# A new order of work, per-bank score waits and slot-wise restacking in two six-layer attention stacks

## What is computed

```
for i in range(NL):                        # NL = 6, B = 2, L = 512, 16 heads of 8 features
    xn = _adaln(x, noise_emb, n1_w[i], n1_b[i])
    q, k, v = split(xn @ qkv_w[i].T);  q, k = _rope(q), _rope(k)
    x = x + _attn(q, k, v, src_mask) @ so_w[i].T           # self attention, 512 keys
    xn = _adaln(x, noise_emb, n2_w[i], n2_b[i])
    q = _rope(xn @ cq_w[i].T);  k = _rope(context @ ck_w[i].T);  v = context @ cv_w[i].T
    x = x + _attn(q, k, v, ctx_mask) @ co_w[i].T           # cross attention, 154 keys
    xn = _adaln(x, noise_emb, n3_w[i], n3_b[i])
    x = x + (gelu(xn @ f1_w[i].T + f1_b[i]) @ f2_w[i].T + f2_b[i])   # DFF = 512
```

## Time and profile before

| | |
|---|---|
| three runs | 3256.78, 3264.88, 3266.14 us; median 3264.88 |
| profiled execution | 3269.45 us, span 3267.6 us |
| busy share of the span | TensorE 89%, VectorE 64%, ScalarE 59%, GpSimd 25% |
| granted TensorE clock | 0.960 of full speed |
| first stack | about 676 to 1877 us |
| second stack | about 1940 to 3145 us |

### The profile page before, as it was taken

How to read it: one execution, slowest core, us unless ns; L and a number is a source line. 1 busy time by engine, 2 the same in 40 slices (tenths; PEclk the granted TensorE clock), 3 DMA queues, 4 the chain that set the end, 5 groups by cost and what they waited for, 6 DMA issues and landing times.

```text
span 3267.6 us, 44859 instructions
## 1 busy us (share of the span) xinstructions
PE 2898.7 (89%) x15719; PEld 1046.8 (32%) x15719; DVE 2098.5 (64%) x3625; ACT 1911.9 (59%) x2677; POOL 828.0 (25%) x1327
## 2 busy tenths in 40 slices
PE   7998999969989898998989857989899898998988
PEld 2474344322323223232222222222323222232237
DVE  4316788548485775948577378577495766848523
ACT  5533444428677584766758435758476575857632
POOL 0003556532222222222222111222222222222201
PEclk9999999979999999999999877999999999999998
DMA  1101000001101111111111101111111111111130
GB/s 46 59 1 26 1 1 1 11 20 38 43 27 38 44 29 41 38 42 36 36 41 33 34 18 30 30 41 34 41 31 40 42 31 37 38 48 29 36 128 7
DMA packets 125514, 110.11 MB, mean 34 GB/s; under 512 B 49982, under 2 KB 116076, under 8 KB 125292
## 3 DMA queue, kind: packets, MB, share of 16 engines
q1 hardware_dynamic: 114924, 97.80, 10.2%
q10 hardware_dynamic: 10368, 9.44, 1.0%
HBM read 41.96 MB, written 0.52 MB: 13 GB/s over the span
## 4 chain that ended last, share of the span: by engine, by line
PE 68%; DVE 17%; ACT 5%; issue 4%; SPq 2%; POOL 2%; DMA 2%; ACTq 0%; DVEq 0%; POOLq 0%
PE ps L524 12%; DVE arena L813 8%; PE ps L469 7%; PE ps L498 3%; PE ps L641 3%; PE ps L656 3%; PE ps L598 3%; PE ps L541 3%; PE ps L1521 3%; PE ps L1509 2%; PE ps L532 2%; PE ps L584 2%; PE ps L553 2%; PE ps L573 2%; PE ps L1467 2%
## 5 line engine op out<-in xcount | busy, mean ns | idle before, releaser
L681 ACT ACTIVATE arena<-ps 128x1024 f32<-128x1024 f32 x960 | 934.6, 1022 | 245.9 <-PE ps L498 235.7
L813 DVE TENSOR_REDUCE arena<-ps 128x1 f32<-128x512 f32 x1536 | 963.9, 683 | 112.5 <-PE ps L469 103.3
L524 PE MATMUL ps<-arena 128*32 128x512 f32 x3840 | 503.2, 605 | 2.1 <-ACT arena L700 0.3
L469 PE MATMUL ps<-arena 49*128 49x512 bf16 x1536 | 309.3, 399 | 154.3 <-DVE arena L813 109.8
L815 DVE TENSOR_REDUCE arena<-ps 128x3 f32<-128x462 f32 (+1 forms) x576 | 305.4, 579 | 139.4 <-PE ps L476 119.0
L498 PE MATMUL ps<-arena 52*128 52x512 bf16 x1920 | 343.0, 385 | 29.8 <-DMA arena<-arena 9.3
L903 POOL TENSOR_TENSOR arena<-arena,zeros 128x16 bf16<-128x16 f32 x192 | 42.3, 220 | 1081.8 <-DVE arena L813 703.2
L469 PEld LDWEIGHTS ps<-arena 49*128 49x128 bf16 x1536 | 74.9, 93 | 545.7 <-DVE arena L813 474.7
L913 POOL TENSOR_TENSOR arena<-arena 128x512 f32<-128x512 f32 x96 | 122.1, 1272 | 388.5 <-ACT arena L713 385.2
L1586 ACT ACTIVATE arena<-ps 128x1024 f32<-128x1024 f32 x96 | 98.1, 1021 | 156.0 <-DVE ps L1671 152.6
L362 PE MATMUL ps<-consts 128*128 128x512 f32 x344 | 166.2, 608 | 23.7 <-DVE arena L2113 23.7
(11 more groups left out here) (389 smaller groups left out, 4351.9 us busy)
## 6 DMA issues: line engine op xcount, KB each, us to landing
arena<-arena SPq DMA_DIRECT2D x720, 64.0 KB
arena<-we_dram SPq DMA_DIRECT2D x24, 578.5 KB, 7.6
arena<-arena ACTq DMA_DIRECT2D x144, 64.0 KB
w<-weights_dram SPq DMA_DIRECT2D x26, 320.0 KB, 3.3
w<-weights_dram SPq DMA_DIRECT2D x13, 512.0 KB, 4.2
arena<-arena SPq DMA_DIRECT2D x384, 6.0 KB
arena<-arena SPq DMA_DIRECT2D x288, 19.2 KB
w<-weights_dram SPq DMA_DIRECT2D x39, 128.0 KB, 2.2
```

The lines of the kernel that those rows point to most:

```text
L469: pe.matmul(s_bank(slot + r), qst[b][rows, idx, P * qt:P * (qt + 1)], kst[b][rows, idx, :], start=True, stop=True).then_inc(s_full, 1)
L524: mm = pe.matmul(bank(7)[32 * j:32 * j + 32, :], v, prob[:, slot, j, :], start=(g % 2 == 0 and kt == 0), stop=(a == 0 and g % 2 == 1 and k ...
L681: act.activation(prob[:, chunk_no(b, a, g, kt) % NPROB, 2 * p:2 * p + 2, :], e_bank(slot).rearrange("p (j n) -> p j n", j=2), ACT.Exp, sca ...
L813: op = ve.tensor_reduce(nmax[:, g % 2, r, n:n + 1], s_bank(slot + r), AX.X, ALU.max, negate=True)
```

## The change

Seven edits, all in the stacks:

1. `st` has one item for each row slot, with two DMAs (four for `u` = 3), and a layer 392 items for 371. The DMAs are the same ones.
2. `ACT_STACKS` has twelve items of two DMAs: ScalarE issues 24 a layer for 12. It waits for the part that the slot needs, so also for the middle and low ones of GpSimd.
3. All places are new. The first score of a layer moves from place 0 to -6. Among the others: `out 1,1` (batch 1's cross output) stood three places before the first score and stands behind the sixth one; `sel 1,1,*` stand behind the second and third score; `f1 1,*` and `f2 1` move from places 13 to 21 to 30 to 34.
4. A self-attention `score` waits for its first bank ahead of the first product and for its second bank ahead of the second one.
5. Fillers: ten for nine, at other items; ahead of a score they wait for one bank only.
6. Other items may have fillers (`exp`, `tail`, `sel`, `proj`, `f2`); of these only two `exp` items have one.
7. On ScalarE and VectorE some pairs of waits of one instruction change their order.

```diff
-PER_LAYER = 371
+PER_LAYER = 392
-    ('score', 0, 0): [[0, 2, 3, 5, 6, 9, 11, 12], [14, 17, 18, 23, 25, 27, 28, 30], [36, 44, 50, 55, 57, 61, 63,
-        66], [69, 71, 77, 79, 82, 85, 89, 92]],
+    ('score', 0, 0): [[-6, -5, -2, 2, 3, 5, 7, 8], [11, 12, 16, 17, 21, 22, 25, 28], [31, 33, 36, 38, 40, 42,
+        44, 48], [56, 58, 71, 73, 74, 76, 82, 84]],
...
-    ('sel', 1): [[214, 254], [362, 364]],
+    ('sel', 1): [[220, 270], [389, 392]],
-    ('out',): [[156, 291], [265, 368]],
+    ('out',): [[177, 309], [278, 398]],
...
-    ('st', 0): [[-22, -2, -4], [-12, -5, -1], [188, 212, 210], [124, 160, 148]],
+    ('st', 0): [[-33, -12, -14, -34, -30, -31], [-23, -28, -19, -20, -15, -16], [203, 219, 214, 212, 208, 206],
+        [183, 145, 178, 129, 156, 153]],
...
-    ('f1',): [[304, 306], [384, 387]],
-    ('f2',): [313, 392],
+    ('f1',): [[319, 322], [422, 424]],
+    ('f2',): [328, 426],
...
-        def restack(eng, b, u, part):
-            for slot in slots_of(u, part):
-                for r in range(2):
...
+        def restack(eng, b, u, slot):
+            part = part_in(u, slot)
+            for r in range(2):
...
-        ACT_STACKS = (("st", 0, 1, 0), ("st", 1, 2, 0))
-        FILL = {("out", 0, 1): 3, ("out", 1, 1): 2, ("f1", 0, 0): 1, ("score", 1, 1, 0, 0): 2, ("center", 0, 2): 1}
+        ACT_STACKS = (("st", 0, 0, 0), ("st", 0, 0, 1), ("st", 0, 1, 1), ("st", 0, 1, 4), ("st", 0, 2, 1),
+                      ("st", 1, 0, 2), ("st", 1, 0, 3), ("st", 1, 1, 1), ("st", 1, 1, 2), ("st", 1, 1, 4),
+                      ("st", 1, 2, 3), ("st", 1, 2, 5))
+        FILL = {('exp', 0, 0, 0, 1, 0): 1, ('exp', 1, 1, 1, 0, 0): 1, ('out', 0, 1): 2, ('score', 0, 0, 1, 1):
+                1, ('score', 0, 0, 1, 3): 1, ('score', 0, 0, 1, 5): 1, ('score', 1, 1, 0, 0): 2, ('var', 0,
+                2): 1}
...
                 if it in FILL:
-                    pe.wait_ge(s_free, z.room("s", it, 2))
+                    pe.wait_ge(s_free, z.room("s", it, 1))
                     fill(it, s_bank(z.use("s", it)[0]))
...
-                pe.wait_ge(s_free, z.room("s", it, 2))
                 if a == 0:
                     idx, qt = 2 * g + n // 4, n % 4
                     for r in range(2):
                         rows = slice(64 * r, 64 * r + K_SCORE)
+                        pe.wait_ge(s_free, z.room("s", it, 1) if r == 0 else floor0(at - 1))
                         pe.matmul(s_bank(slot + r), qst[b][rows, idx, P * qt:P * (qt + 1)], kst[b][rows, idx, :],
                                   start=True, stop=True).then_inc(s_full, 1)
                     return
+                pe.wait_ge(s_free, z.room("s", it, 2))
...
-                    act.wait_ge(part_hi, z.after("hi", ("hi", b, u), it))
-                    restack(act, b, u, part)
+                    act.wait_ge((part_hi, part_mid, part_lo)[part_in(u, slot)], z.after("hi", ("hi", b, u), it))
+                    restack(act, b, u, slot)
```

More of the change, by code:

```diff
@@ new lines @@
+    ('sel', 0): [[139, 161], [299, 301]],
+    ('sel', 1): [[220, 270], [389, 392]],
+    ('inv', 0): [[146, 164], [300, 303]],
+    ('inv', 1): [[224, 271], [391, 393]],
+    ('out',): [[177, 309], [278, 398]],
+    ('center',): [[-59, 184, 311], [39, 284, 402]],
+    ('var',): [[-55, 188, 312], [43, 289, 407]],
+    ('apply',): [[-48, 194, 315], [46, 290, 412]],
+    ('proj',): [[-41, -36, 198, 86], [53, 57, 302]],
+    ('hi',): [[-35, -29, 200, 128], [59, 62, 304]],
+    ('st', 0): [[-33, -12, -14, -34, -30, -31], [-23, -28, -19, -20, -15, -16], [203, 219, 214, 212, 208, 206],
+        [183, 145, 178, 129, 156, 153]],
@@ L139 @@
+    ('st', 1): [[61, 70, 68, 60, 67, 81], [77, 78, 65, 89, 69, 90], [305, 313, 316, 306, 307, 308]],
+    ('ktail',): 211,
+    ('vals',): [4, 133, -7],
+    ('f1',): [[319, 322], [422, 424]],
+    ('f2',): [328, 426],
+    ('gain',): [-82, -13, 314],
+    ('biasf',): 291,
+    ('load',): {'cout': 419, 'cross': 350, 'ffn': 634, 'n0': 241, 'n1': 189, 'n2': 558, 'self': 259, 'sout':
+        346},
 }
@@ L175, in steps @@
     if kind == "st":
[L176 to L177 removed]
+        return {"c": 64} if item[2] == 3 else {("k" if item[2] == 1 else "q") + str(item[1]): 32}
     if kind == "load":
@@ L492, in exp @@
                 slot, at = z.use("e", it)
+                if it in FILL:
+                    pe.wait_ge(e_free, z.room("e", it, 1))
+                    fill(it, e_bank(slot)[:, 0:S])
                 if p == 0 and kt == 0:
@@ L589, in proj @@
                 slot, at = z.use("s", it)
+                if it in FILL:
+                    pe.wait_ge(s_free, z.room("s", it, 1))
+                    fill(it, s_bank(slot))
                 if u == 3:
@@ L964, in stack @@
             def stack(it):
-                _, b, u, part = it
+                _, b, u, slot = it
                 if it not in ACT_STACKS:
-                    sp.wait_ge((part_hi, part_mid, part_lo)[part], z.after("hi", ("hi", b, u), it))
-                    restack(sp, b, u, part)
+                    sp.wait_ge((part_hi, part_mid, part_lo)[part_in(u, slot)], z.after("hi", ("hi", b, u), it))
+                    restack(sp, b, u, slot)
             def load(it):
```

108 lines of the change are left out of this document (48 added, 60 removed), and 2 rows, old and new, of the table PLACES.

## The result

The changed kernel takes 3286.75 us (median of four runs, 3280.57 to 3296.74), the kernel before 3260.83 us in runs on the same chip. The ratio is 1.0102, 95% interval 1.0064 to 1.0140: **slower by 1.0%, where 1.0% faster was forecast**. The two profiled executions differ by only 11 us, because two parts that the change does not touch happened to be quicker after: the last block took 111.4 us against 123.5 (its clock was at half speed for 6.8 instead of 27.3 us), and the blocks ahead of the first stack took 2.7 us less. Counted from the last addition to `x` ahead of a stack to the stack's last `f2`, the first stack takes 1211.0 us for 1200.0 and the second 1220.8 for 1205.8. Together they are 26 us longer, as much as the medians are apart.

The account below looks back on a forecast made before the run. VectorE was taken to pace R1, TensorE R2 and R3, dependences R4. From the profiled 3269.45 us it took 24.6 (order), 3 (starts) and 7 (clock): 3234.9, stated as 3233 us on the median's scale, range 3190 to 3290.

Parts of the forecast that it names:

- Splitting a score's wait at nothing: Self-attention scores waiting for each bank separately: no effect taken; bounds 48 us gained, up to 56 us lost.
- R4: Layer stretch from batch 1's first cross-attention score reduction: 41.72 us before, 39.1 forecast, with the restack landing earlier.
- R3: Layer stretch from batch 0's first cross-attention score reduction: 44.93 us before, 43.7 forecast, with TensorE setting the pace.
- The starts: Restack at each stack's start, SyncE issuing 16 DMAs for 18: 1.5 us a stack, 3 us in all.
- rival B: At the turn of layers the restack does not land earlier: 3265 us as a median, no change; chance 0.18.
- R1: Layer stretch from batch 0's first self-attention score reduction: 53.43 us before, 52.0 forecast, still bounded by VectorE.
- Before, 5.4 us stood above its busy time; with six `exp` less in the way I keep 3.2: In R1, the time above VectorE's busy 48.8 us was taken as 3.2 us, giving 52.0.
- R2: Layer stretch from batch 1's first self-attention score reduction: 50.77 us before, 54.0 forecast, TensorE and ScalarE about equal.
- Rival A: ScalarE becomes the bound of R2, making the kernel slower: about 3291 us; chance 0.22.
- I take nothing: ScalarE's 12 further DMA issues a layer, covered by its idle time in R4 and R1; without cover 7.8 us.
- The clock: Half-speed dips at later layers' first score group: 7 us gained, half of 14.6; bounds 15 gained, 22 lost.
- The sum: Four stretches total 188.8 us, 2.05 us a layer less, 24.6 for twelve; with starts and clock, 3233 us.

## Why the prediction was wrong, by its own steps

**Splitting a score's wait at nothing: right, but its sign was wrong.** Two runs, either way, show nothing. The prediction had also said that if the listed wait fell by 40 us or more, the split would be misjudged. It fell by 79.6 us, and the products' busy time rose by 79.7: that list can't tell.

**R4 and R3: right in mechanism.** R4 39.1 forecast, 37.6 measured; R3 43.7 and 43.9. SyncE needed 11.07 us for 16 DMAs where I had taken off 1.5 from 13.33. **The starts**, from the restack's begin to the first score, went from 15.0 to 12.8 us and from 15.1 to 12.8: 4.6 us in all where I had 3. But a fixed price of 0.74 us for each DMA taken off SyncE was not the right working. 13.33 us for 18 holds 1.3 us in which SyncE stood waiting for a part, and without a stand a DMA takes it 0.65; with 14 on ScalarE instead of twelve nothing was gained, as the two were high parts, for which nobody waited. Here ScalarE also takes a middle part's slot of either stack, and SyncE doesn't stand. So rival B is out, and with it the rule of the Trainium skill that I weighed (DMA: Bandwidth & Descriptors, "Issuing engines are not separate DMA queues"), that what issuing from several engines saves is usually small. For these DMAs it is not: R1's last group with batch 1's ten DMAs on SyncE shows 6.14 us of waiting for issue.

**"Before, 5.4 us stood above its busy time; with six `exp` less in the way I keep 3.2": this step failed.** R1's busy times came out as worked out: TensorE 48.24 (48.1 forecast), VectorE 48.90 (48.8). But 7.45 us stood above VectorE's. A stretch of 50 us was too long here for "this engine sets the pace". By groups of eight scores the busier of TensorE and VectorE has, before and in the changed kernel without split:

| | R1's groups | sum | length | above | R2's groups | sum | length | above |
|---|---|---|---|---|---|---|---|---|
| before | 11.08, 12.88, 13.99, 11.15 | 49.1 | 53.4 | 4.3 | 10.00, 10.67, 12.30, 14.82 | 47.8 | 50.8 | 3.0 |
| after | 10.63, 11.60, 16.14, 13.17 | 51.5 | 56.35 | 4.8 | 9.94, 10.68, 13.14, 19.06 | 52.8 | 55.1 | 2.3 |

The rows of the table that carry most of it, R1's second to fourth group and R2's last one before, then R2's last one in the changed kernel without split:

```profile
910.57:926.25 15.68, 12.88 (x51) 3.89 (x51) 11.85 (x19) 9.08 (x13) 1.14 (x5) 1.00 0.02 5
926.25:940.46 14.21, 12.85 (x73) 3.41 (x77) 13.99 (x24) 11.52 (x15) 7.43 (x7) 1.00 0.20 57
940.46:951.68 11.22, 10.18 (x71) 3.46 (x67) 11.15 (x20) 7.91 (x12) 3.10 (x7) 1.00 0.25 71
986.90:1002.46 15.56, 14.82 (x100) 3.79 (x98) 12.00 (x21) 13.77 (x17) 4.41 (x8) 1.00 0.19 53
...
980.64:1000.38 19.74, 19.06 (x121) 4.66 (x119) 13.35 (x22) 16.41 (x21) 6.68 (x10) 1.00 0.18 53
```

These floors grew by 7.5 us, the two stretches by 7.2. What stands above the floors didn't change: 7.3 and 7.1 us. A part of 2.0 us of the growth is unevenness alone, which sums over a stretch hide: batch 1's `f1` and `f2` fill R1's third group, where TensorE has 16.1 us of work beside VectorE's 13.9, and the turning and splitting of batch 1's queries and keys, which the third group held before, stands in the fourth, where VectorE now has 13.2 us for 11.2. The same rows could be had of the kernel before, and the items of each group counted in the new list. That "above" stays as it was would have given 56 us for R1 in place of 52.0. One run supports this way of reading in part: moving the 5 us of `f1` and `f2` into a group as full raises the floors of R1 by 1.4 us (52.5 to 53.9, both with the split) and R1 by 3.4 at full clock, the 1.73 us for ScalarE among them. The direction is right, but here what stands above the floors grew by 2.0, so that it stays is no rule. And these floors leave out what ScalarE issues: with 24 DMAs in the old order for 14 they grow by 0.9 us over R1 and R2, and the two stretches by 4.5. In the changed kernel ScalarE is busy 6.87 us in R1's fourth group and issues for 6.80, 13.67 of 14.25 us, more than VectorE's 13.17.

**R2 54.0: near, 55.1.** TensorE had 52.22 us (51.3 forecast), ScalarE 47.8, 87% where I had said over 90; even with the 1.4 us of its two DMA issues, which don't count as busy, it is 49.2, below its 51.6. Rival A, ScalarE as R2's bound, has the size (3291 forecast, 3287 measured) but not the mechanism: R2 is TensorE's.

**"I take nothing", ScalarE's twelve further issues under the cover of its idle time: failed, in a way that the changed kernel hides.** In the old order they cost 59 us, of the 94 us (7.8 a layer) that I had named as their price without cover. Idle time of an in-order queue is no cover, if what it waits for (TensorE's products) waits in turn for what stands behind the DMAs. What they cost inside the new order wasn't measured by itself: taken away, batch 1's restack comes late and more is lost. The 0.5 us by which ScalarE's busy and issue time exceeds VectorE's busy time in R1's fourth group is all that the rows show of them in R1; that they cost no more is argued, not shown.

**The list of what moved left out batch 1's own restack.** I worked out the turn of layers for batch 0, to the tenth, and for batch 1 only said that 18 of 24 issues lie there under cover. The same working with batch 1's first score gives 43.6 us instead of 33 from batch 0's first score to the restack's begin, with batch 1's first score only 3 us later. The order takes 4.1 us from R4 and gives R1 the `sel`, `out` and fillers that stood there; what is then pushed out is batch 1.

**The clock: 7 us forecast, none came.** Four dips of 10.2 us at the first group became four of 3.4 and two of 13.7, 41 us of half speed in both kernels, and the mean above the undisturbed layer is 2.8 us a layer (195.8 for 193.0) for 2.1 before. What the Trainium skill says in TensorE: Matmul & The Clock Gate, "A second HAM failure mode: psum-queue depth-cycling", that micro-idles of a bank ring let the clock oscillate, gave zero for this term, and zero came; it is not shown here that the ring is the cause of the dips.

**The sum.** Per layer I had -2.05 us and got +2.15, so 4.2: R1 4.2, R2 1.3, R3 0.2, R4 -1.5. Times twelve that is 50 us, and the clock a further 7 or more; the starts gave back 1.6. The median was off by 54. That it still lies inside the stated range, and 4 us from rival A's number, is luck: neither the forecast's mechanism nor A's is what happened.

What stays open: why what stands above the floors is 7 us in one case and grows in another, and which of the new order's placements in R1 could be kept. The two that I tried, earlier, are worse, and no run takes single items of the new order over into the old one.

## What to carry to other kernels

Before a bound is read from busy sums, cut the stretch down (here to groups of eight scores, some twelve microseconds; no other length was tried), and count the issuing of DMAs in with an engine's busy time. The sum of the larger time by group, plus what stood above it before, would have been the better forecast here: 56 us for R1 instead of 52.0. An issue of a DMA on a computing engine isn't covered by that engine's idle time but only by the slack of whatever stands behind it in its queue: twelve more cost 1.8%. Moving some off SyncE helps only where they are what its queue's end waits for: two or four more high parts gained nothing that can be told. When one batch's chain is pulled forward, work out the other batch's restack to the same detail.

## What the runs showed that I had not expected

- Ten fillers a layer, which nobody reads, are worth 1.9% in one order, and the same ten in the old order are no better than the nine there. Where TensorE is busy matters more than how much.
- One DMA of 64 KB between parts of SBUF keeps SyncE's sequencer 0.65 us (24 in 15.67 us) and ScalarE's 0.64 to 0.70 (two in 1.28, six in 4.22, both in R1's fourth group of the changed kernel), while the 16 DMA engines are busy at 0.36 on average in that group.
- A wait that vanishes from the list of waits (109.8 to 30.2 us) may only have been covered by busy time, here of the pair's first product, which had run beside the second; busy and idle time together, 463.6 us before and 478.5 after for L469 and L473, show that no time left.
